# Second feed-forward of a four-block transformer kernel: softplus in one activation, written orders, row halves

## The reference, cut to what matters

```python
logits = gelu(xf @ w_r1 + b_r1) @ w_r2 + b_r2          # 8 experts
top_p, top_i = top_k(softmax(logits), 2); top_p /= sum(top_p)
v = zeros; integrated = xf
for _ in range(2):
    ctx = concat([integrated, v])
    # the shared expert and each chosen expert e, width 64 inside:
    ctrl = gelu(ctx @ w1[e] + b1[e]) @ w2[e] + b2[e]   # 3 x 128 wide
    alpha, beta, gate = sigmoid(ctrl[0]), softplus(ctrl[1]), sigmoid(ctrl[2])
    v_e = alpha * v - beta * (integrated - mu); x_e = integrated + 0.1 * gate * v_e
    x_next, v_next = weighted sums of x_e, v_e (sigmoid(shared_weight) for the shared one)
    halt = sigmoid(gelu(x_next @ w_h1 + b_h1) @ w_h2 + b_h2)
    refined = gelu(x_next @ w_f1 + b_f1) @ w_f2 + b_f2
    integrated += halt * refined * integration_weight; v = v_next
```

## Time and profile before

| | before |
|---|---|
| median of three runs | 953.72 us |
| the profiled execution's own time | 955.74 us |
| its span | 954.0 us |
| PE busy | 739.0 us, 77% |
| DVE busy | 629.7 us, 66% |
| ACT busy | 531.1 us, 56% |
| POOL busy | 211.9 us, 22% |
| granted TensorE clock, mean | 0.879 |

### The profile page before, as it was taken

How to read it: one execution, slowest core, us unless ns; L and a number is a source line. 1 busy time by engine, 2 the same in 40 slices (tenths; PEclk the granted TensorE clock), 3 DMA queues, 4 the chain that set the end, 5 groups by cost and what they waited for, 6 DMA issues and landing times. The chain is left out here.

```text
span 954.0 us, 14468 instructions
## 1 busy us (share of the span) xinstructions
PE 739.0 (77%) x4720; PEld 415.6 (44%) x4720; DVE 629.7 (66%) x1861; ACT 531.1 (56%) x1376; POOL 211.9 (22%) x161
## 2 busy tenths in 40 slices
PE   4599973399975776877783559995899999969987
PEld 2266652166653222322331236664533666644322
DVE  3699957399963557686786569986532656634543
ACT  2398841198843775775674149882367655522211
POOL 7702004100004345364364630001010000000000
PEclk9699995599995987888896759998899999988999
DMA  7992040420000000000000190000000000000000
GB/s 285 181 345 68 3 67 1 103 31 2 2 2 0 0 1 0 0 1 0 1 0 0 26 173 2 2 3 23 1 0 1 1 1 1 1 0 1 1 0 23
DMA packets 22060, 32.29 MB, mean 34 GB/s; under 512 B 1761, under 2 KB 15713, under 8 KB 21217
## 3 DMA queue, kind: packets, MB, share of 16 engines
q1 hardware_dynamic: 21984, 31.36, 13.1%
HBM read 21.39 MB, written 9.96 MB: 33 GB/s over the span
## 5 line engine op out<-in xcount | busy, mean ns | idle before, releaser
L715 ACT ACTIVATE RING<-RING,NMX 128x256 f32<-128x256 f32 x384 | 190.6, 500 | 54.1 <-DVE NMX L1444 53.5
L1444 DVE CUSTOM_DVE_ANT_0 RING<-bank,ADJM 128x256 f32<-128x256 f32 x384 | 143.4, 413 | 22.7 <-DMA scratch<-RING 21.7
L1018 PE MATMUL bank<-W,RING 128*128 128x128 f32 x768 | 120.3, 281 | 15.7 <-ACT RING L727 14.0
L495 POOL TENSOR_TENSOR small<-small 128x8 f32<-128x8 f32 (+2 forms) x13 | 17.6, 1360 | 463.8 <-DVE small L1335 463.8
L1018 PEld LDWEIGHTS bank<-W,RING 128*128 128x128 f32 x768 | 91.3, 145 | 28.1 <-ACT RING L715 24.5
L998 PE MATMUL bank<-ARENA 128*128 128x256 bf16 x384 | 77.5, 289 | 28.8 <-DMA ARENA<-scratch 23.6
L1456 DVE COPY RING<-bank 128x512 f32<-128x512 f32 x144 | 98.6, 686 | 1.2 <-PE bank L1018 0.8
L857 PE MATMUL bank<-XT,W 128*128 128x512 f32 (+3 forms) x138 | 78.0, 706 | 7.2 <-ACT XT L611 5.1
L857 PE MATMUL bank<-ARENA 128*128 128x512 f32 (+2 forms) x164 | 62.2, 522 | 23.8 <-DVE ARENA L1537 10.2
L857 PE MATMUL bank<-ARENA,W 128*128 128x512 f32 (+4 forms) x104 | 54.4, 648 | 27.7 <-DVE ARENA L1657 10.9
L590 POOL TENSOR_TENSOR ARENA<-ARENA,RING 128x512 f32<-128x512 f32 x38 | 59.8, 1583 | 67.4 <-DVE RING L1627 35.5
(11 more groups left out here) (240 smaller groups left out, 1395.6 us busy)
## 6 DMA issues: line engine op xcount, KB each, us to landing
scratch<-ARENA SPq DMA_DIRECT2D x18, 256.0 KB, 3.1
ARENA<-scratch SPq DMA_DIRECT2D x6, 768.0 KB, 10.6
W<-in_weights SPq DMA_DIRECT2D x1, 2564.0 KB, 21.2
scratch<-RING SPq DMA_DIRECT2D x36, 64.0 KB, 3.2
ARENA<-scratch SPq DMA_DIRECT2D x12, 192.0 KB, 3.7
scratch<-RING SPq DMA_DIRECT2D x18, 128.0 KB, 2.7
ARENA<-scratch SPq DMA_DIRECT2D x6, 384.0 KB, 7.0
W<-in_weights SPq DMA_DIRECT2D x2, 1024.0 KB, 13.8
```

Source lines behind the costliest of these rows:

```text
L715: nc.scalar.activation(P_OF(n)[:, q * S:(q + 1) * S], S_OF(n)[:, q, :], ACT.Exp, bias=NMX[:, 2 * t + q:2 * t + q + 1], scale=-1.0, accum_o ...
L1018: mm = nc.tensor.transpose(bk[:, o:o + P], P_OF(n)[:, i:i + P], ident)
L1444: nc.vector.tensor_tensor_reduce(out=S_OF(n)[:, q, :], in0=SBANK(n)[:, q * S:(q + 1) * S], in1=ADJM[:, b, q, :], scale=-1.0, scalar=BIG, o ...
```

## The change: what it does

- Softplus is one activation out of PSUM, into one of 13 slots; clamp, Exp, Ln and maximum are gone.
- The units are called by (pass, expert); the shared expert NE comes first. All of ScalarE's banks are one ring of six (0, 1, 2, 3, 6, 7), emptied in order. Loops over groups give way to an order written out for each engine.
- WE2P is gone; `control` multiplies 64 rows, the lower half for even experts and NE, the upper half for odd ones. GpSimd's memsets and copies for WE2P, XN and HIDR go.
- VectorE adds some pairs of terms (PAIR1, PAIR2); GpSimd adds what is left, in a written order.
- The first hidden products come ahead of the router and between it and the weight rows; these are products with the identity on 24 rows, copied by VectorE.
- `top2` finds both experts by comparing and reducing over all tokens at once. ScalarE's Exp reads LOG. The sigmoid of the shared weight is made from a Tanh.
- GpSimd's `roots()` of attention 1 stand ahead of `masks(1)`.
- Eight transposes and eight residual additions at the end become two banks of four transposes and two additions.

```diff
 PIECES = [(0, S), (S, 2 * S), (2 * S, 4 * S)]
 QK_AT = [2, 9, 12]
+UN = (NE,) + tuple(range(NE))
+SP_SLOTS = 13
+PAIR1 = ((0, 2, 6), (4,), (), (6,))
+PAIR2 = ((2, 4, 6), (4, 6), (4, 6), (4, 6))
+ADDS1 = ((0, 4, 2, 5, 6), (0, 1, 2, 3, 4, 6, 7), (0, 1, 2, 3, 4, 5, 6, 7), (0, 1, 2, 3, 4, 5, 6))
...
+        def SP_OF(p, e):
+            return SLOTS[(9 * p + UN.index(e)) % SP_SLOTS]
...
+        class Mixed:
+            def __init__(self, banks, full):
+                self.banks, self.full, self.freed, self.n = banks, full, [], 0
+            def fill(self, eng, emptied, value):
+                k = len(self.banks)
+                if len(self.freed) >= k:
+                    eng.wait_ge(*self.freed[-k])
+                self.freed.append((emptied, value))
+                return bank[self.banks[(len(self.freed) - 1) % k]]
...
+        def sum1_free(eng, p, e):
+            if p < NC:
+                eng.wait_ge(s_t2[p], nth(e))
+            if e - 1 in PAIR1[p]:
+                eng.wait_ge(s_p1[p], PAIR1[p].index(e - 1) + 1)
+            else:
+                eng.wait_ge(s_a1[p], 1 if e == NE else ADDS1[p].index(e) + 1)
...
+            roots()
             masks(1)
-            roots()
             root()
...
-            pool.wait_ge(s_ld[2], 16)
-            link(nc.gpsimd.memset(WE2P, 0.0))
-            pairs = w("we2").rearrange("p (j f) -> p j f", f=3 * D)
-            nc.gpsimd.tensor_copy(WE2P[0:HID1, 0::2, :], pairs[0:HID1, :, :]).then_inc(s_pad, 1)
-            nc.gpsimd.tensor_copy(WE2P[HID1:P, 1::2, :], pairs[HID1:P, 0:NE // 2, :]).then_inc(s_pad, 1)
-            nc.gpsimd.memset(HIDR[HID1:P, 4, :], 0.0).then_inc(s_pad, 1)
...
-            for u in range(FU):
-                p, e = divmod(u, NE + 1)
-                c = p % NC
-                sum1, term2 = (VEL, GT_OF(u)) if p < NC else (BACC, AT_OF(u))
-                for acc, term, s_term, s_sum in ((sum1, SP_OF(u), s_t1, s_a1), (GACC, term2, s_t2, s_a2)):
-                    pool.wait_ge(s_term, u + 1)
-                    if e == 0:
-                        nc.gpsimd.tensor_copy(acc[:, half(c)], term).then_inc(s_sum, 1)
-                    else:
-                        pool.wait_ge(s_sum, u)
-                        nc.gpsimd.tensor_tensor(acc[:, half(c)], acc[:, half(c)], term,
-                                                ALU.add).then_inc(s_sum, 1)
...
+            def add1(p, e):
+                h, k = half(p % NC), ADDS1[p].index(e)
+                acc = VEL if p < NC else BACC
+                if e in PAIR1[p]:
+                    pool.wait_ge(s_p1[p], PAIR1[p].index(e) + 1)
+                else:
+                    pool.wait_ge(s_t1[p], nth(e))
+                if k >= 1:
+                    pool.wait_ge(s_a1[p], k)
+                nc.gpsimd.tensor_tensor(acc[:, h], SP_OF(p, NE) if k == 0 else acc[:, h], SP_OF(p, e),
+                                        ALU.add).then_inc(s_a1[p], 1)
...
+            add2(0, 0)
+            add1(0, 0)
+            add2(0, 1)
+            add1(0, 4)
+            add1(0, 2)
...
+            def betas(p, es):
+                for e in es:
+                    src = r6.take(act)
+                    i = 9 * p + UN.index(e) - SP_SLOTS
+                    if i >= 0:
+                        sum1_free(act, i // 9, UN[i % 9])
+                    nc.scalar.activation(SP_OF(p, e), src[:, :], ACT.Softplus,
+                                         bias=be2[:, e, 1:2]).then_inc(s_sp[p], 1)
+            def gates(p, es):
+                for e in es:
+                    src = r6.take(act)
+                    if 1 <= p <= NC:
+                        sum2_free(act, p - 1, e)
+                    elif p > NC:
+                        act.wait_ge(s_t1[p - 1], nth(e))
+                        act.wait_ge(s_t2[p - 1], nth(e))
+                    nc.scalar.activation(GT_OF(e), src[:, :], ACT.Tanh, bias=BE2H[:, 3 * e + 2:3 * e + 3],
+                                         scale=0.5).then_inc(s_gt[p], 1)
...
-                if 3 * i + 3 < FU:
-                    exponentials(i + 1)
+            nc.scalar.activation(EXPL, LOG, ACT.Exp).then_inc(s_el, 1)
+            betas(0, (NE, 0, 1))
+            hidden(1, (3, 4))
+            gates(0, (NE, 0, 1))
+            betas(0, (2, 3, 4, 5))
+            gates(0, (2, 3, 4, 5, 6, 7))
+            betas(1, (NE,))
+            betas(0, (6, 7))
+            betas(1, (0, 1, 2, 3, 4, 5))
+            gates(1, (NE, 0, 1, 2, 3, 4, 5, 6, 7))
+            refine(0)
+            halting(0)
+            betas(1, (6, 7))
+            hidden(2, (0, 1, 2, 3, 4))
+            gates(2, (NE, 0, 1, 2, 3))
+            alphas(2, (NE,))
+            gates(2, (4, 5))
+            alphas(2, (0, 1))
+            betas(2, (NE, 0, 1, 2, 3))
             refine(1)
+            alphas(2, (2, 3, 4, 5))
             halting(1)
-            ra.n += r3.n
+            betas(2, (4, 5))
+            gates(2, (6, 7))
+            betas(2, (6, 7))
+            hidden(3, (0, 1, 2, 3, 4))
+            alphas(2, (6, 7))
+            gates(3, (NE,))
+            alphas(3, (NE,))
+            gates(3, (0, 1))
+            alphas(3, (0, 1))
+            gates(3, (2, 3))
+            betas(3, (NE, 0, 1, 2, 3))
+            alphas(3, (2, 3))
+            gates(3, (4, 5, 6, 7))
+            alphas(3, (4, 5))
+            betas(3, (4, 5, 6, 7))
+            refine(2)
+            alphas(3, (6, 7))
+            halting(2)
+            refine(3)
+            halting(3)
...
+            def control(p, part, es, emptied):
+                for e in es:
+                    j, r = e // 2, HID1 * (e % 2)
+                    f = 3 * D * j + part * D
+                    pe.wait_ge(s_h[p], j + 1)
+                    bk = r6.fill(pe, emptied, nth(e))
+                    nc.tensor.matmul(bk[:, :], w("we2", f, f + D, rows=HID1, row0=r),
+                                     HIDR[r:r + HID1, j, half(p % NC)], start=True, stop=True).then_inc(s_f6, 1)
...
+            hidden(0, (0, 1, 2))
+            router()
+            hidden(0, (3, 4))
+            hidden(1, (0, 1, 2))
+            betas(0, (NE,))
+            betas(0, (0, 1))
+            hidden(1, (3, 4))
+            gates(0, (NE,))
+            gates(0, (0, 1))
+            betas(0, (2, 3))
+            weight_rows()
+            weights(0, (0, 1))
+            betas(0, (4, 5))
...
+            refine(0)
+            halting(0)
+            weights(1, (4, 5))
+            betas(1, (6, 7))
+            hidden(2, (0, 1, 2, 3, 4))
+            weights(1, (6, 7))
+            gates(2, (NE, 0, 1))
...
-                for k, sel in enumerate((SEL, SELB)):
-                    chain(nc.vector.tensor_tensor(sel, iota, IDXF[:, :, k:k + 1].to_broadcast([P, NT, NE]),
-                                                  ALU.is_equal))
-                settle()
+                dve.wait_ge(s_log, n)
+                link(nc.vector.tensor_scalar(TMP8, LOG, 0.0, float(NE), ALU.is_lt, ALU.mult))
+                link(nc.vector.tensor_tensor(TMP8, TMP8, iota, ALU.add))
+                link(nc.vector.tensor_reduce(IDXF[:, :, 0], TMP8, AX.X, ALU.min))
+                link(nc.vector.tensor_tensor(SEL, iota, IDXF[:, :, 0:1].to_broadcast([P, NT, NE]), ALU.is_equal))
+                link(nc.vector.scalar_tensor_tensor(REST8, SEL, -BIG, LOG, ALU.mult, ALU.add))
+                link(nc.vector.tensor_reduce(MX2[:, :, 0], REST8, AX.X, ALU.max))
...
+            def first(p, es):
+                for e in es:
+                    sp = SP_OF(p, e)
+                    if e < NE:
+                        wgt = rw.take(dve)
+                        dve.wait_ge(s_sp[p], nth(e))
+                        nc.vector.tensor_tensor(sp, sp, wgt[:, :], ALU.mult).then_inc(s_t1[p], 1)
+                    else:
+                        dve.wait_ge(s_sp[p], nth(e))
+                        nc.vector.tensor_scalar(sp, sp, SWC, None, ALU.mult).then_inc(s_t1[p], 1)
+            def second(p, es):
+                for e in es:
+                    gt = GT_OF(e)
+                    dve.wait_ge(s_t1[p], nth(e))
+                    dve.wait_ge(s_gt[p], nth(e))
+                    nc.vector.scalar_tensor_tensor(gt, gt, 1.0, SP_OF(p, e), ALU.add, ALU.mult).then_inc(s_t2[p], 1)
...
+            def pair1(p, e):
+                dve.wait_ge(s_t1[p], nth(e + 1))
                 if p < NC:
-                    if e < NE:
...
+            pair1(0, 6)
+            second(0, (7,))
+            pair2(0, 6)
+            first(1, (NE, 0, 1))
+            x_next(0)
+            second(1, (NE, 0))
+            first(1, (2, 3))
+            integrate(0)
+            second(1, (1,))
+            first(1, (4, 5))
+            second(1, (2, 3, 4))
+            pair1(1, 4)
+            second(1, (5,))
+            pair2(1, 4)
...
+            betas(3, (6, 7))
+            pair1(3, 6)
+            alphas(3, (6, 7))
+            pair2(3, 6)
             x_next(3)
+            integrate(2)
             integrate(3)
```

(81 more changed lines are left out.)

547 lines of the change are left out of this document (286 added, 261 removed).

## The result

The changed kernel takes **865.62 us** (863.47 to 866.31, 4 runs), the kernel before 953.55 (951.46 to 954.16, 4 runs): a ratio of 0.908 [0.907, 0.909], 88 us less. The profiled execution took 863.47 us. The forecast was 881 in a range of 860 to 911. The time lies in the range, but at the value of rival (b), 865, in which the written order fits almost exactly; the forecast's own case was 15 us too slow.

The account below looks back on a forecast made before the run. It took hand-overs between three engines to bound the second feed-forward. Terms: -66.9 (feed-forward), -5.8 (attention 1's roots), +0.2 (last top-2) = -72.5 us from 955.74, giving 883.2, in medians 881; range 860 to 911.

Parts of the forecast that it names:

- rival (b): Second feed-forward: the written order fits exactly, stalls of 5 instead of 21.5 us, kernel 865 us; chance 0.15.
- the forecast's own case: Whole kernel: 72.5 us less, 881 us in medians; chance 0.54 with some us around it.
- Rival (e): Second feed-forward: softplus at 1.1 us each, ScalarE 127 us and partly on the path, kernel 889 us; chance 0.05.
- (d): Second feed-forward: 64-row halves don't overlap and TensorE stays at 1.2 GHz, kernel slower at 976 us; chance 0.03.
- (c): Second feed-forward: fifty row changes drain TensorE, 0.28 us each, with TensorE on the path, kernel 895 us; chance 0.05.
- my 102 to 122 us: TensorE's forecast work in the second feed-forward: 102 us at 2.4 GHz, 122 at the loop's mix of clocks.
- seam 2: Second feed-forward's loop from 318: VectorE's 115 us, a 5.5 us stall and 16 us allowance, `x_next(3)` ending at 454.5.
- Rival (a): Second feed-forward: the hand-over stays the bound, VectorE busy 69%, +30 us, kernel 912 us; chance 0.17.
- The roots: Attention 1: GpSimd's roots ahead of the masks let XN start at about 162.8; -5.8 us, bounds 3 and 6.2.
- theory A: Attention 1, roots runs: TensorE's stall goes and it keeps its upper clock, worth 7 to 8 us.
- Seam 1: Second feed-forward's start: first multiply by a token weight at 318 instead of 325.2, 7 us earlier.
- Pairs: Second feed-forward: fourteen pair additions new on VectorE at 1.0 us each, 14 us, ends 10 and 23.

Follow-up runs that it names:

- e1: Kernel before with softplus as one activation and top-2 by compare, old order and banks kept: 923.42 us, ratio 0.968.
- e4: Changed kernel with Exp and Ln in place of softplus, same order, clamp left out: 891.62 us, ratio 0.934.
- e3: Changed kernel with the experts' second-layer products on 128 rows, except the shared expert's: 873.06 us, ratio 0.915.
- e2: Kernel before with GpSimd's roots ahead of the masks at attention 1, nothing else: 946.31 us, ratio 0.992.
- e6: Changed kernel with GpSimd's roots behind the masks at attention 1, as before: 874.06 us, ratio 0.917.
- e12: Changed kernel with all 64 additions on VectorE, no pairs and none on GpSimd: 857.97 us, ratio 0.900.
- e5: Changed kernel without VectorE's pair additions, GpSimd adding all 64 terms: 869.16 us, ratio 0.913.
- e8: Changed kernel with each of GpSimd's 50 additions on 256 of its 512 columns: 846.67 us, ratio 0.888.

## Why the prediction was right, and which term was off

**The reading held.** I read the loop as "a circle over three banks" that goes when softplus is one eviction and the order is written out. After it, VectorE is the bound at 90%, above the 80% that I had named as the sign. Softplus 0.691 us against 0.687 taken; 21 table loads of 1.283 us in the stage, as counted (9 softplus; Gelu 3 at L857, 3 at L895, 1 at L846; Tanh 3 at L879, 1 at L888; one Exp at L909). Rival (e) is out by the first (its own terms give 126 us of ScalarE, not 127). VectorE up to `integrate(3)` 112.9 us against 117. But e1, which shortens that circle to a product and a softplus and keeps the old order, takes only 26.9 of the loop's 73.4 us: the circle is one part of the hand-over, not all of it. And e4 corrects the emphasis: the 29.5 us that ScalarE sheds here are worth 24 us of loop, though the sum let VectorE alone set the loop.

**The halves.** Four 64-row products take 1.99 us, as taken from attention's row; two alone take 1.13, not 0.9 to 1.0. From the timeline, TensorE:

```profile
308.22 1.99 PE L1274 MATMUL bank<-ARENA,W 64*128 64x512 f32 x8
...
310.14 0.60 PE L1250 MATMUL bank<-RING,W 24*128 24x512 bf16 x2
...
342.02 0.60 PE L1250 MATMUL bank<-RING,W 24*128 24x512 bf16 x2
342.55 1.13 PE L1274 MATMUL bank<-ARENA,W 64*128 64x512 f32 x4
...
345.41 1.02 PE L1264 MATMUL bank<-ARENA,W 128*128 128x512 f32 x2
346.27 1.02 PE L1261 MATMUL bank<-ARENA,W 128*128 128x512 f32 x2
```

The halves overlap, which rules out (d). For the drain of (c), I had read "no drain" from records that overlap (342.55 against 342.62), as in the earlier trace rows; but the ends of matmul records are modelled, and only the starts are measured. By the starts, 128-row groups without a change of rows follow each other after 0.86 us, and two pairs of 64-row products reach the next kind of rows after 1.92 us, where twice 0.86 is 1.72. So a change costs some 0.2 us, not nothing and not far from the 0.28 of (c); with 45 changes in the loop I estimate 9 us of TensorE. (c) fails at its other condition: TensorE is not on the path. It is busy for 98.2 of the loop's 122.7 us.

That 98 must not be held against my 102 to 122 us, which were for all 144 products and the weight products. Over the three stretches (275.0 to 440.7) these take 127.9 us, above both values: the half-row products 0.61 each, as forecast at the mix of clocks, the 54 others 61.8 / 54 = 1.14 each, where I had 0.85 and 1.04. Of their 320 instructions the loop holds at most 271.

**The mis-sized term** is the allowance in seam 2: "for banks, slots, weight products and waits on ScalarE I add 16 us, a choice". VectorE's idle time in the loop is 12.7 us in sum, of which 6.7 are the written stall (5.5 predicted); the allowance is worth 6, not 16. With 110 us of work instead of 115 the loop ends after 122.7 us against 136.5: 10 less for the allowance, 5 less for the work, 1.2 more for the stall. That is 13.8 of the 18.9 us by which `integrate(3)` came earlier than forecast (440.7 against 459.6). The reason I gave for the allowance, TensorE close beside VectorE, was wrong in effect: even at 119.5 us of TensorE, in e3, the kernel lost only 7.4.

Rival (b) has the measured time, but in part by luck: it wanted stalls of 5 us in sum, and VectorE stands 12.7. Less VectorE work, an earlier start of the loop and a tail 1 us shorter made up for the difference. Rival (a) is out, with VectorE at 90% and not 69%. Its "any idle stretch lets its clock fall" does not hold as it stands either: at attention 1 the granted clock was 0.50 from 170.4 to 173.0 behind the pause of 6.22 us, but 1.00 from 162.7 to 165.3 in the changed kernel, with pauses of 0.47 and 0.62 us.

**The roots**: -5.8 predicted, with bounds of 3 and 6.2; e2 and e6 measured 7.8 and 8.7. I had bounded the gain by TensorE's idle 6.22 us, but TensorE's own products ahead of that wait moved too: they end at 162.85 instead of 164.24, of which 0.7 came from upstream. What went is VectorE's whole wait for the roots, 7.19 us before and 8.00 in e6. So the upper bound was no bound. The clock, theory A's reason, shows in the first products (two transposes 0.44 us at a granted 1.00, 0.66 at 0.50 before) but not in the sum: from the first XN on, attention 1 lasts as long with the pause as without it (last section).

**Seam 1**: -7 predicted, -8.9 measured. The router ran at 289.59 in 1.95 us at a granted clock of 1.00, where I had the 3.6 us of the kernel before, at 0.50. VectorE's chain then waited 3.58 us for ScalarE's Exp and its table load (298.69), which I had not foreseen.

**Pairs**: 14 us taken, 9.1 + 6.7 = 15.8 busy. The price was right and the reading of its use was not: I noted that GpSimd stretches VectorE's operations up to 1.631 us, and kept it as a fixed price of each operation. It is GpSimd's price, and it can be removed (e12).

What stays open: of the 88 us, taken out one at a time from the changed kernel, softplus is 26, the ring of six cut to three banks 9.6, roots 8.7, halves 7.4 and pairs 3.8, 56 in sum. The other 32 us are put down to the written order and what goes with it; it was not undone by itself, and parts taken out singly need not add up.

## What to carry to other kernels

When three engines are each busy about 70% of a stage, find the circle of waits first. Once it is cut, let the busiest engine's time set the stage and add little: here a list written out in full left 6 us of idle time beside its one built-in stall. Before giving VectorE's sums to GpSimd, compare the same VectorE operation with and without a GpSimd operation beside it. If both engines work on SBUF, the time that VectorE loses may be more than the sum itself costs there.

## What the runs showed of the hardware

**GpSimd and VectorE hold each other up on SBUF operands.** The changed kernel at 370 us, GpSimd and then VectorE:

```profile
370.29 1.64 POOL L625 TENSOR_TENSOR ARENA<-ARENA,RING 128x512 f32<-128x512 f32 x1 [1.82 <-DVE RING L1828]
371.90 1.72 POOL L638 TENSOR_TENSOR ARENA<-ARENA 128x512 f32<-128x512 f32 x1
373.57 1.72 POOL L625 TENSOR_TENSOR ARENA<-ARENA,RING 128x512 f32<-128x512 f32 x1
```

```profile
370.13 0.68 DVE L1820 SCALAR_TENSOR_TENSOR ARENA<-ARENA 128x512 f32<-128x512 f32 x1
370.73 1.76 DVE L1828 TENSOR_TENSOR RING<-RING,ARENA 128x512 f32<-128x512 f32 x1
372.41 1.75 DVE L1820 SCALAR_TENSOR_TENSOR ARENA<-ARENA 128x512 f32<-128x512 f32 x1
374.09 0.67 DVE L1809 SCALAR_TENSOR_TENSOR ARENA<-ARENA,bank 128x512 f32<-128x512 f32 x1
```

The same `alphas` takes 0.68 us where it starts ahead of the addition (370.13) and 1.75 where one is running (372.41); the one that reads a bank (374.09) takes 0.67 beside a running addition. A GpSimd addition takes 1.26 us at its shortest and 1.64 to 1.72 here. The Trainium skill (SBUF — State Buffer, "Who interferes with whom") says that a VectorE instruction with two SBUF inputs contends with a GpSimd one that reads SBUF, and that the later of them waits; the rows agree. In sum, as an estimate: at e12's 104.3 / 173 = 0.603 us each, 123 instructions are 74.2 us, so the 50 additions of GpSimd cost VectorE 35.8 us, 0.72 each, where one on VectorE costs 0.60. In e5 it is (101.65 - 109 x 0.603) / 64 = 0.56 each, so the price depends on how the two queues meet. That the additions are the cause, and not VectorE's own queue, is what e8 and e12 show.

**A higher granted clock that bought nothing.** Attention 1 from its first XN to the layer norm behind it, in the changed kernel and in e6, in which TensorE had stood 7 us just before:

```profile
161.60:275.10 113.50, 91.67 (x1000) 64.66 (x998) 92.37 (x366) 81.53 (x296) 15.25 (x17) 0.94 0.14 29
```

```profile
170.20:283.20 113.00, 93.32 (x990) 65.40 (x990) 90.36 (x365) 80.76 (x294) 1.26 (x1) 0.90 0.15 30
```

Without the pause the clock is 0.94 instead of 0.90, and the stretch is as long: the masks' 15 us of GpSimd, now inside it, cost nothing visible either.
